# Attention pieces stored side by side, so that a slot's six row groups load as runs of 8, 16 and 24 partitions

## The reference

```
# layer 0: q is the layer norm of x, k and v are the context; scale 1/sqrt(8)
# layer 1:
qh = q.reshape(B, h, d, Tq); kh = k.reshape(B, h, d, Tk); vh = v.reshape(B, h, dv, Tk)
qn = _l2norm(qh, axis=-2); kn = _l2norm(kh, axis=-2)
qk = ALPHA * jnp.einsum('bhdq,bhdk->bhqk', qn, kn)
sm = jax.nn.softmax(qk, axis=-1)
out = jnp.einsum('bhqk,bhdk->bhdq', sm, vh)
```

## Time and profile before

| | us |
|---|---|
| median of 3 runs | 4081.2 |
| lowest, highest | 4078.17, 4097.26 |
| profiled execution | 4080.67 |
| its span | 4078.6 |
| granted TensorE clock, mean | 0.852 |
| PE, DVE, ACT, POOL busy | 2872.7, 2306.6, 1423.1, 801.9 |

### The profile page before, as it was taken

The page is one execution under the profiler, slowest core; times in us unless marked ns, Lnnn a source line. Parts: engine busy times, 40 slices in busy tenths (PEclk is TensorE's granted clock), DMA queues, the critical chain, the costliest instruction groups (busy, mean ns, idle before and its releaser), DMA issues. The chain is left out here.

```text
span 4078.6 us, 60992 instructions
## 1 busy us (share of the span) xinstructions
PE 2872.7 (70%) x19886; PEld 1814.7 (44%) x19886; DVE 2306.6 (57%) x4671; ACT 1423.1 (35%) x2783; POOL 801.9 (20%) x1136
## 2 busy tenths in 40 slices
PE   5288874465999934499255893488869725999994
PEld 5123323222555514133123672244447524888883
DVE  7589976475777774333587886655559630000003
ACT  5267761352322212499134551011125301111110
POOL 3011110573333310011100330000013232111110
PEclk7599995798999965699568997799989857999997
DMA  7655520997222251553000431100024121121113
GB/s 245 156 112 119 119 67 7 352 366 257 80 81 79 80 173 44 111 133 75 23 0 16 141 108 43 36 12 10 10 77 141 49 89 51 44 77 52 51 56 124
DMA packets 271080, 394.34 MB, mean 97 GB/s; under 512 B 59457, under 2 KB 199982, under 8 KB 270560
## 3 DMA queue, kind: packets, MB, share of 16 engines
q1 hardware_dynamic: 243936, 321.16, 27.9%
q0 software_dynamic: 25152, 68.22, 4.8%
q10 hardware_dynamic: 1728, 1.57, 0.3%
HBM read 231.94 MB, written 164.44 MB: 97 GB/s over the span
## 5 line engine op out<-in xcount | busy, mean ns | idle before, releaser
L2582 POOL DMA_INDIRECT rows_out<-e_out,e_tr_dest x224 | 234.5, 1047 | 871.7 <-DVE e_out L2995 521.4
L1184 ACT ACTIVATE a_pt<-a_psS 128x512 f32<-128x512 f32 x512 | 277.6, 595 | 173.2 <-PE a_psS L1082 168.7
L1206 DVE TENSOR_REDUCE a_mx_sb<-a_psM 128x4 f32<-128x1024 f32 x256 | 293.9, 1216 | 35.1 <-PE a_psM L1065 33.8
L2995 DVE COPY e_out<-e_psD 128x512 f32<-128x512 f32 x40 | 27.7, 692 | 492.0 <-PE e_psD L2963 491.8
L2763 PE MATMUL e_psG<-e_wgu,e_yT 128*128 x576 | 274.5, 599 | 27.0 <-ACT e_yT L2791 24.2
L1096 PE MATMUL a_psV<-a_pt,a_vt 128*18 128x256 f32 x4096 | 292.2, 388 | 1.2 <-issue 0.8
L2963 PE MATMUL e_psD<-e_w,e_hT 128*128 128x256 f32 x1280 | 289.8, 386 | 0.0
L2952 PE MATMUL e_psH<-e_yT,e_w 128*128 128x256 f32 x1280 | 284.5, 381 | 1.6 <-issue 0.8
L2963 PEld LDWEIGHTS e_psD<-e_w,e_hT 128*128 128x128 f32 x1280 | 245.5, 194 | 33.2
L2952 PEld LDWEIGHTS e_psH<-e_yT,e_w 128*128 128x128 f32 x1280 | 244.2, 191 | 35.5 <-issue 2.1
L1082 PE MATMUL a_psS<-a_qa,a_ka 50*128 50x256 bf16 (+1 forms) x2048 | 194.3, 279 | 87.5 <-DMA a_ka<-n_pieces 49.0
(11 more groups left out here) (368 smaller groups left out, 5811.7 us busy)
## 6 DMA issues: line engine op xcount, KB each, us to landing
kbd<-e_bgu SPq DMA_DIRECT2D x64, 512.0 KB
cr_kbd<-kbd SPq DMA_DIRECT2D x64, 512.0 KB, 3.4
a_qa<-q_pieces SPq DMA_DIRECT2D x384, 64.0 KB
rows_in<-zeros POOLq DMA_DIRECT2D x36, 522.0 KB, 8.1
e_xin<-rows_in SPq DMA_DIRECT2D x144, 128.0 KB
vbd<-e_bd SPq DMA_DIRECT2D x64, 272.0 KB
cr_vbd<-vbd SPq DMA_DIRECT2D x64, 272.0 KB, 2.7
cb_rows<-rows_out SPq DMA_DIRECT2D x32, 512.0 KB, 4.4
```

The lines of the kernel that those rows point to most:

```text
L1184: act.activation(pt[:, probs(t, h), b, :, :], psS[:, unit(t, h, b) % S_BANKS, :].rearrange("p (k c) -> p k c", k=KC), ACT.Exp, scale=scale ...
L1206: dve.tensor_reduce(mx[:, t % 2, :, h, :], psM[:, k % 2, :, :].rearrange("p b (f c) -> p b f c", f=2), AX_X, ALU.max).then_inc(ring_read, 1)
L2582: pool.indirect_dma_start(out=self.rows_out[0:limit, :], out_offset=bass.IndirectOffsetOnAxis(ap=self.dest[:, t:t + 1], axis=0), in_=rows, ...
```

## The change

The three DRAM tensors go from `[piece, half, group, head, row, tile, column]` to `[group, half, head, piece, row, tile, column]`: the three pieces of one head, 8 rows each, lie side by side, for q in the order high, middle, low and for k and its normalised form in the order low, middle, high. A store then covers both halves: 128 partitions, 512 KB, one per piece and group in place of two; the counts that wait for stores follow (`n_store`). A load takes one, two or three neighbouring pieces at once: 8, 16 and 24 partitions, 64, 128 and 192 KB, six per operand and slot in place of twelve. The row groups in `qa` and `ka` hold the same pieces as before, and the matmuls are the same.

```diff
-    n_store = PIECES * 2
+    n_store = PIECES
@@ phase_front
-                def store(pieces, parts, g, piece, stored):
-                    for b in range(2):
-                        sp.dma_start(pieces[piece, b, g].rearrange("h d t c -> (h d) t c"),
-                                     parts[HALF * b:HALF * b + HALF, g % 2, piece, :, :]).then_inc(stored[g % 2], 16)
+                def store(pieces, parts, g, piece, at, stored):
+                    sp.dma_start(pieces[g, :, :, at].rearrange("b h d t c -> (b h) d (t c)"),
+                                 parts[:, g % 2, piece, :, :].rearrange("p t c -> p (t c)")).then_inc(stored[g % 2], 16)
...
-                        store(k_pieces, kp, g, piece, k_stored)
+                        store(k_pieces, kp, g, piece, PIECES - 1 - piece, k_stored)
...
-                        store(q_pieces, qp, g, piece, q_stored)
+                        store(q_pieces, qp, g, piece, piece, q_stored)
...
-                        for b in range(2):
-                            sp.dma_start(n_pieces[piece, b, g].rearrange("h d t c -> (h d) t c"),
-                                         np[HALF * b:HALF * b + HALF, piece, :, :]).then_inc(n_stored, 16)
+                        sp.dma_start(n_pieces[g, :, :, PIECES - 1 - piece].rearrange("b h d t c -> (b h) d (t c)"),
+                                     np[:, piece, :, :].rearrange("p t c -> p (t c)")).then_inc(n_stored, 16)
@@ ahead of phase_split
-Q_SLOTS, K_SLOTS = (0, 0, 1, 0, 1, 2), (0, 1, 0, 2, 1, 0)
-SLOTS = len(Q_SLOTS)
+RUNS = (1, 2, 3)
+SLOTS = sum(RUNS)
@@ phase_split: its store changes as q's in phase_front
@@ phase_attend
-    LOADS = 4 * SLOTS
+    LOADS = 4 * len(RUNS)
...
                 for b in range(2):
-                    for k, piece in enumerate(Q_SLOTS if operand == "q" else K_SLOTS):
-                        at = HALF * b + HD * k
-                        eng.dma_start(dst[at:at + HD, m, :, :, :].rearrange("r h t c -> r h (t c)"),
-                                      src[piece, b, g, :, :, first:first + SLOT_TILES].rearrange("h d t c -> d h (t c)")).then_inc(qk_loaded[m], 16)
+                    at = HALF * b
+                    for run in RUNS:
+                        run_pieces = slice(0, run) if operand == "q" else slice(PIECES - run, PIECES)
+                        eng.dma_start(dst[at:at + HD * run, m, :, :, :].rearrange("r h t c -> r h (t c)"),
+                                      src[g, b, :, run_pieces, :, first:first + SLOT_TILES].rearrange("h i d t c -> (i d) h (t c)")).then_inc(qk_loaded[m], 16)
+                        at += HD * run
@@ flamingo_decoder
-    q_pieces, k_pieces, n_pieces = (dram(n, [PIECES, 2, TILES // GROUP, HEADS, HD, GROUP, DIM], BF16) for n in ("q_pieces", "k_pieces", "n_pieces"))
+    q_pieces, k_pieces, n_pieces = (dram(n, [TILES // GROUP, 2, HEADS, PIECES, HD, GROUP, DIM], BF16) for n in ("q_pieces", "k_pieces", "n_pieces"))
```

More of the change, by code:

```diff
@@ L740, in _ @@
                         sp.wait_ge(p_ready, i * PIECES + (piece + 1))
-                        for b in range(2):
-                            sp.dma_start(pieces[piece, b, i].rearrange("h d t c -> (h d) t c"),
-                                         parts[HALF * b:HALF * b + HALF, i % 2, piece, :, :]).then_inc(stored[i % 2], 16)
+                        sp.dma_start(pieces[i, :, :, piece].rearrange("b h d t c -> (b h) d (t c)"),
+                                     parts[:, i % 2, piece, :, :].rearrange("p t c -> p (t c)")).then_inc(stored[i % 2], 16)
                     if src is not None and i + 2 < NG:
```

## The result

The kernel after takes 4061.3 us (median of 7, 4052.6 to 4067.1), the kernel before beside it 4081.2 (median of 7): ratio 0.9942, interval 0.9925 to 0.9959. That is a gain of 17 to 31 us, where 38 was forecast. The runs were taken on several chips, each beside the kernel before, so the ratios compare and the medians only roughly.

A forecast was written before the change was run, and what follows sets the result against it. No single engine bounds the kernel; DVE bounds the first attention's middle, ScalarE the second's, and savings lie in waits for loads. 12.9 + 12.1 + 10.0 + 2 + 1 = 38.0 us off 4081.2 gives 4043, range 4030 to 4066.

The forecast's parts named there:

- Items 1 and 2: Prologues of the first and second attention: PE starts earlier behind fewer load packets, gains 12.9 and 12.1 us.
- I take 10% under the present pace: Time per packet in the two prologues: 85 and 80 ns, from 94.6 and 88.7 before.
- 227 packets: Packets the busiest engine handles before PE starts an attention: 70 + 17 + 70 + 70, in place of 341.
- its bounds, 132 and 55 ns per KB: Limits on the pace, from load rates in the profile before: 132 ns at 188 to 191, 55 at 1736 to 1752.
- Item 3: First attention, PE's 12.1 us wait for shift 1 behind q and k of slot 2: gain 10.0 us.
- Item 4: PE's other six waits for shift rows, 5.6 us together: gain 2 us, range 0 to 4.
- Item 5: Fewer stores at the ends of front (0.7 us) and split of q (0.3): together 1 us, range 0 to 1.5.
- Item 6: SP issues 384 loads fewer; outside the prologues and the 12.1 us wait this gains nothing, no wait stands later.
- rival C: Second attention becomes bound by its loads, sixteen engines disturbing each other to 125 ns: 41 us slower, 4122; chance 0.05.
- A: Rival: the 24-row load stays on eight engines, 275 packets in place of 341: gain 19 us, 4062; chance 0.08.
- B: Rival: sources set the rate, pace rises from 94.6 to 142 ns, all waits stay: 4080; chance 0.11.
- D: Rival: taller loads relieve more, pace 55 to 60 ns, both prologues at their floors: gain 46 us, 4035; chance 0.20.

The follow-up runs named there:

- m2: Kernel timing loads alone, 1 KB packets, varying destination step and height: 121 ns a packet for 8 rows, 124 for 16, 77 for 24, 82 for 64.
- e2: The kernel after, with k of slot 0 issued by SP ahead of q of slot 1 instead of by ScalarE: 4041.9 us, ratio to before 0.9917.
- e3: The kernel after, with head rows 4.5 KB apart in DRAM instead of 4: 4052.6 us, ratio to before 0.9946.
- e5: The kernel after, with e2's order, e3's pitch and DVE's fills of buffers 1 to 3 behind its last setup instruction: 4037.5 us, ratio 0.9906.
- e6: e5, with each operand's loads in the second attention waiting for those before them from slot 2 on: 4077.5 us, ratio to before 0.9985.
- e9: e5, with one wait in the second attention that allows up to three operands under way: 4039.3 us, ratio to before 0.9924.
- e7: e5, with the first piece stored twice and each half loaded by two 24-row loads: 4032.8 us, ratio to before 0.9880.
- e8: e7 with e6's wait, and the shift rows of tile 1 issued ahead of k of slot 2: 4031.2 us, ratio to before 0.9870.
- m1: Kernel timing loads alone in nine patterns: 43.5 us for 8-row loads in the old layout, 26.6 for runs of 8, 16 and 24 in the new.
- e1: The kernel after, new layout and single stores kept, but every run split back into loads of 8 rows: 4070.9 us, ratio to before 0.9981.
- e4: The kernel before, with k of slot 0 issued by SP ahead of q of slot 1: 4048.6 us, ratio to before 0.9957.
- H: Segment of m1: 8-row loads with each source row 8 KB contiguous, against the old layout's 8-row loads: 47.4 us against 43.5.
- F: Segment of m1: runs of 8, 16 and 24 rows with a source pitch of 4.5 KB instead of 4: 26.5 us against 26.6.
- E: Segment of m1: 8-row loads with source rows at a pitch of 4.5 KB instead of 4: 31.0 us against 43.5.

## Why the prediction was right, and where it was off

The path, the items, the places and the packet counts were right; the pace was not.

Items 1 and 2, the starts: 7.2 and 4.7 us of the 12.9 and 12.1 forecast. **The step that was off is the pace**, "I take 10% under the present pace", with its reason, "Taller loads reach more partitions at once, more engines read at once". With 227 packets, counted rightly, (26.7 - 1.7) / 227 = 110 ns and (27.2 - 1.7) / 227 = 112 ns, where 85 and 80 were taken. It rose by 16 and 26% over before's. In m2's numbers an operand by packets, a sixth from 8-row loads, a third from 16-row and half from 24-row ones, gives 121 / 6 + 124 / 3 + 77 / 2 = 100 ns: the 16-row load puts sixteen engines onto sixteen neighbouring partitions and gains nothing per packet. The starts of all runs, by the same working, agree: 105 to 112 ns in the twelve with runs of 8, 16 and 24 (after, e2, e3, e5, e6, e9), 75 to 84 in the four with 24 rows only (e7, e8). What the numbers don't settle is why before stood at 95 and 89, so the rise is explained only as far as 100 ns, and m1 shows none (43.5 us / 432 packets = 101 ns, 26.6 / 280 = 95).

The pace of 8-row loads is the open end. Their six starts (before, e1, e4) range from 78 to 110 ns. Inside the kernel before it moves further, with the same rows and partitions; q1 at 189 to 204 and at 1740 to 1747:

```profile
q1 hardware_dynamic: 1195, 1.09, 56.6%
q1 hardware_dynamic: 1321, 1.21, 55.1%
```

That is 114 and 47 ns a packet at one share, about nine engines' worth, so the engines were no less busy when the packets were short. (The prediction had both ends as its bounds, 132 and 55 ns per KB.) So neighbouring partitions alone don't make a packet slow; what else must come together is not shown.

Item 3, the long wait: 7.7 us of 10.0, for the same reason. SP issued q of slot 2 at 175.15, PE went on at 193.37: (193.37 - 175.15 - 1.7) / 144 = 115 ns instead of 99.

Item 4, the other shift waits: 5.6 us before, 1.2 after, a gain of 4.4 against 2. Items 3 and 4 together gave 12.1, and the body's 11.9 agrees.

Item 5: the front came out 1.1 us shorter (0.7 expected), which is no more than e4's unchanged front differs from before's. The split can't be told from the mid's scatter of 5 us either, from which the other 3.3 came.

Item 6, "outside items 1 to 3 this is nothing": wrong by 3.8 us. The loads do fit in the second attention, as said against rival C, and nothing waits for them. But its first 60 us let the queue fill up to the four buffers, on all sixteen engines, where eight had been left free before, and PE stood for 3.5 us. That the backlog goes with it is what e9 shows (and e6, e7 and e8: no stall with a shorter one). Sixteen busy engines are not needed: e1, with 8-row loads, has a stall of 0.6 us.

The traces hint at what PE waited for. They have packets of kind "instruction", 16 KB each on queue q8. Here is q8 at after's second stall, from 1714.2 to 1715.9, and at e5's, from 1692.1 to 1694.1:

```profile
q8 instruction: 1, 0.02, 5.9%
q8 instruction: 1, 0.02, 5.6%
```

Such a packet ends 1.5 to 1.9 us before PE goes on in each of the seven stalls above 0.4 us of the second attention (one in e1, e3 and e5, two in after and e2). The gap to the q8 packet before it is 20.7 us in e5 (first stall 3.7 us), 19.2 in after (1.5), 19.1 in e2 (2.1) and 18.7 in e1 (0.6). At the same place it is 13.6 to 16.9 us in the seven other kernels, which don't stall there (e3 does at its next packet). That fits a PE that waits for instructions, and instructions that come late because their packets stand behind the loads. It is the likely reading and not more: no row shows where a packet waits before it starts, and no run delays these packets alone.

Of the rivals A came nearest in time (4062) with the wrong mechanism: q10 carried 1680 packets, twelve engines for 24 rows, where A had eight. B, a pace that rises as the packets fall, was half true: it rose by 16 and 26%, where B had 50. But a rate set by the sources is not borne out: H, F and e3 gained nothing from another source, and e7 moved the same bytes faster (only E, for 8-row loads, speaks for the source). D's pace of 55 to 60 ns did not come; e7 reached its time (4032.8 us) with other edits and 78 ns. The slower case C didn't come either: no load is late in the middle of the second attention, though 157 packets in 15.7 us leave 100 ns for one and the starts ran at 110.

## What to carry to other kernels

Count the packets on the busiest engine, but take the price of one from a load of the same height and partition spacing, and as a range: alone, a packet cost 109 to 124 ns in loads of 8 and 16 neighbouring partitions and 77 to 82 in those of 24 to 64, while in the kernel before 8-row loads ran at anything from 47 to 114. Before shortening a transfer that someone waits for, see what stands between it and its issue: one operand moved ahead of another, which nobody waited for yet, brought as much as the whole change. A prefetch with free buffers should be bounded to what the pace needs: one operand was too few at 106 ns a packet (e6, 40 us more than before in that stage), and all four buffers too many (e5, 6 us more than e9).

## What the runs showed of the hardware

- Loads alone, 1 KB packets: 121 ns a packet for 8 neighbouring partitions, 124 for 16, 77 for 24, 78 for 32, 82 for 64 (m2), 47 for 128 (m1). Eight rows a step of two or more apart took 49 to 52 ns, with the engines partly idle.
- Loads of 8 neighbouring rows ran at 114 ns a packet in one attention of before and at 47 in the other, at the same DMA share. With what the pace moves is open.
- Two queues at once are served in turn, packet by packet (118 and 119 packets in 3 us), so the second does not make the first one's data come sooner: one queue, in order, brought PE's start 8 us forward (e2).
- TensorE stood 0.5 to 3.7 us in the midst of a run of matmuls, with no semaphore to wait for, while a long backlog of loads was under way, and went on 1.5 to 1.9 us behind the end of a 16 KB packet of instructions.
- Behind the stall of 3.7 us the granted clock fell to 0.50 (1.2 GHz) for about 6 us (e5); behind stalls of up to 2.1 us it stayed at 1.00 (after, e2).
